# A post-norm transformer layer on eight cores: the context tile is copied out of PSUM ahead of its normalisation, and the down-projection weights are loaded from another queue

## The chip, the cores and the metric

One Trainium2 chip, all 8 cores, one launch. The cores do not exchange data. Each core owns 2048 of the 16384 tokens, half a sequence. In attention it takes four of the sixteen heads' weights and one batch after another (a batch is a wave), with the queries of its half and all 4096 keys. The metric is device time in microseconds (us) of the slowest core; less is better. TensorE (PE), VectorE (DVE), ScalarE (ACT), GpSimd (POOL) and SyncE (SP) are the engines. PE's clock has two levels, 1.2 and 2.4 GHz; a granted clock of 1.00 in a row is 2.4 GHz and 0.50 is 1.2 GHz.

## The reference

```python
x = L0_attn_query                                # [4, 4096, 2048] f32
x = layernorm(x + attention(x, Wqkv, Wproj, bproj))
x = layernorm(x + ffn(x, gate_up_packed, gate_up_scales, down_packed, down_scales))

# attention: 16 heads of 128, the sequence read as 16 groups (b*nh), softmax over keys
mixed = x @ Wqkv.T;  attn = softmax(q @ k.T / sqrt(128));  ctx = attn @ v;  out = ctx @ Wproj.T + bproj
# ffn: weights are 4-bit codes, eight in an int32, with a scale per 128 inputs
gate, up = split(x @ dequant(gate_up).T);  h = silu(gate) * up        # 5632 wide
y = h @ dequant(down).T;  y / sqrt(mean(y*y) + 1e-6)
```

## The kernel before

Every engine has its own instruction stream. The same Python walks through the whole program five times, once per engine, and emits only that engine's instructions; semaphores with counts worked out beforehand order them. So an instruction's place in its engine's stream follows from its place in the Python text, and a wait holds up all that stands behind it in that stream.

**Phase A** (to about 3650 us) runs four waves. A wave first makes K, V and Q for its tokens (L496, L514, L550), then does attention for four head slots. A slot has four query chunks of 512 queries. A query chunk walks over 32 key tiles in 16 pairs: PE makes two score tiles (`emit_S`, L587), ACT takes their exponential (L613), and PE multiplies them with V (L634) into two PSUM banks, `pCV[0]` and `pCV[1]`. Each bank holds two query tiles of 129 columns, the 129th being the sum of the exponentials. There is only this one pair of banks for the context, so the first V matmul of the next query chunk (`p == 0`) has to wait until the last one is out of them. DVE takes the reciprocals (L652, two instructions) and then writes `ctxg` by four multiplications (L663); POOL stores `ctxg` (L673). PE's wait at L627 is for the fourth of these multiplications.

Between these steps stand calls of `pace()`, twice in a query chunk: in its middle and between its last V matmul and the context work on DVE. Each adds one or two items of dequantisation: POOL loads packed weights (L285), DVE unpacks (L318, L324, L333) and scales them (L344), PE transposes (L365), ACT copies (L375), and POOL stores the bf16 weights to DRAM (L390). DVE is two items ahead of PE in this.

**Phase B** does the output projection and the first layer norm.

**Phase C** (from about 4400 us) runs over 4 chunks of 512 tokens. A chunk first does 44 gate and up steps (L966, L972), each on 1 MB of weights `wbC` loaded by SP (L947) into four buffers, with the chunk's 2 MB of input `h1tc` loaded by SP ahead of them (L935). Then come two passes (`pp`) of the down projection, each over 256 tokens: 44 steps (`ic`) of 8 matmuls (L1040) on 512 KB of weights `wdC`, again in four buffers. A pass ends with the second norm for its two token tiles on DVE (L1057 to L1136), and POOL stores each tile (L1145).

SP's stream in a chunk is: `h1tc`; 44 loads of `wbC`, each waiting for the step four before it; then for each pass two loads of `h1r` (L1008), of which the one for token tile t waits for the finished norm of tile t-2 (`cyt`, L1007). POOL's stream is: for each pass 44 loads of `wdC` (L1020), each waiting for the step four before it, then the two stores of the output, each waiting for its tile's finished norm. So POOL's `wdC` loads for the second pass stand behind the stores of the first.

Of the kernel before, what the change touches and what calls it, by code (L numbers as in the profile page):

```python
# [8 lines left out]
F32 = mybir.dt.float32  # L9
# [102 lines left out]
def build_nc(cfg):  # L112
# [56 lines left out]
    with contextlib.ExitStack() as TOP:  # L169
# [66 lines left out]
        with contextlib.ExitStack() as SA:  # L236
# [8 lines left out]
            Pt = EA(nc.sbuf_tensor("Pt", [128, 4, QCH], BF16))  # L245
            ctxg = [EA(nc.sbuf_tensor(f"ctxg{i}", [128, QT, 128], BF16)) for i in range(2)]
            rcp = EA(nc.sbuf_tensor("rcp", [128, 4], F32))
            sqb = EA(nc.sbuf_tensor("sqb", [128, 2, 128], BF16))
            bscal = EA(nc.sbuf_tensor("bscal", [1, 8], F32))
            bscal_bf = EA(nc.sbuf_tensor("bscal_bf", [1, 1], BF16))  # L250
# [146 lines left out]
            def phaseA(w: W):  # L397
# [44 lines left out]
                def pace(final=False):  # L442
                    us[0] += 1
                    tgt = n_items if final else us[0] * n_items // TOTAL_US
                    deq_vec_upto(min(n_items, tgt + DEQ_FIFO - 1))
                    deq_pe_upto(tgt)
# [24 lines left out]
                for wav in range(4):  # L471
# [98 lines left out]
                    for l in range(NL):  # L570
# [23 lines left out]
                        for qc in range(NQCH):  # L594
                            gqc = slot_idx * NQCH + qc
                            for p in range(NPt):
# [26 lines left out]
                                if w.on("tensor"):  # L623
                                    t = w.eng
                                    t.wait_ge(sems["sSP"], w.c("sSP"))
                                    if p == 0:
                                        t.wait_ge(sems["sCv"], w.c("sCv"))  # L627
                                    for tloc in range(2):
                                        ti = 2 * p + tloc
                                        inst = None  # L630
                                        for qt in range(QT):
                                            bank = pCV[qt // 2]
                                            off = (qt % 2) * 129
                                            inst = t.matmul(bank[:, off:off + 129],  # L634
                                                            Pt[:, (gpi % 2) * 2 + tloc,
                                                               qt * 128:(qt + 1) * 128],
                                                            V_wave[:, l, ti, 0:129],
                                                            start=(ti == 0), stop=(ti == KT - 1),
                                                            skip_group_check=True)
                                        w.inc(inst, "sPV", 1)  # L640
                                else:
                                    w.note("sPV", 2)
                            pace()
                            if w.on("vector"):
                                v = w.eng
                                v.wait_ge(sems["sPV"], w.c("sPV"))
                                if gqc >= 2:
                                    w.pwait("sCd", gqc - 2)
                                v.wait_ge(sems["sCv"], w.c("sCv"))
                                for b2 in range(min(2, QT)):  # L650
                                    nq = min(2, QT - 2 * b2)
                                    w.inc(v.reciprocal(  # L652
                                        out=rcp[:, b2 * 2:b2 * 2 + nq],
                                        in_=pCV[b2][:, 128:128 + 129 * nq:129]), "sCv", 1)
                                v.wait_ge(sems["sCv"], w.c("sCv"))
                            else:
                                w.note("sCv", min(2, QT))
                            for qt in range(QT):
                                bank = pCV[qt // 2]
                                off = (qt % 2) * 129  # L660
                                if w.on("vector"):
                                    v = w.eng
                                    w.inc(v.tensor_scalar(out=ctxg[gqc % 2][:, qt, :],  # L663
                                                          in0=bank[:, off:off + 128],
                                                          scalar1=rcp[:, qt:qt + 1], scalar2=None,
                                                          op0=ALU.mult), "sCv", 1)
                                else:
                                    w.note("sCv", 1)
# [234 lines left out]
        with contextlib.ExitStack() as SC:  # L903
# [15 lines left out]
            def phaseC(w: W):  # L919
# [10 lines left out]
                for ch in range(NTC):  # L930
# [69 lines left out]
                    for pp in range(NPAIR):  # L1000
# [12 lines left out]
                        for ic in range(ITC):  # L1013
                            kd = (ch * NPAIR + pp) * ITC + ic
                            par = ic % 4
                            if w.on("gpsimd"):
                                gp = w.eng
                                if kd >= 4:
                                    gp.wait_ge(sems["sDm"], w.m(f"dm{kd-4}", "sDm"))
                                w.pinc(gp.dma_start(out=wdC[par][:],  # L1020
                                                    in_=d_wdn[ic * 128:(ic + 1) * 128, :]),
                                       "sDw", kd, 4)
                            else:
                                w.pnote("sDw", kd, 4)
# [200 lines left out]
```

## Time and profile before

| | us |
|---|---|
| median of 2 runs | 6830.76 |
| lowest, highest run | 6687.31, 6974.21 |
| profiled execution | 6665.64 |
| its span, slowest core (core 1) | 6664.0 |
| spans of the eight cores | 6625.4 to 6664.0 |
| PE busy, share of the span | 4675.4, 70% |
| DVE busy | 2361.9, 35% |
| ACT busy | 2039.8, 31% |
| POOL busy | 612.8, 9% |

The profiled execution is one run; the two timed runs lie 21.7 and 308.6 us above it. A busy share is an average over phases that have different limits, so it doesn't say what a step is worth; for that one looks at what each stretch of idle PE time waited for.

### The profile page before, as it was taken

To read this page: it belongs to the slowest core of one execution; us is meant where nothing else is said; L and a number is where in the kernel's file an instruction comes from. 1 tells how busy PE (TensorE), PEld (TensorE's weight loads), DVE (VectorE), ACT (ScalarE), POOL (GpSimd) and SP (SyncE) were. 2 spreads that over 40 slices of the span, in tenths; PEclk is the share of its full clock that TensorE was granted. 3 is DMA by queue.
4 is the path that set the end of the run, shared out by engine and by line. 5 is a ranking of instruction groups with operands and counts; after the bars stand their busy time and mean duration, and the time that the engine had idled before them with its cause. 6 is when DMAs were issued, how large, how long until landed. Compare 5 with 4: busy or idle time off the path is not lost.

```text
span 6664.0 us, 82502 instructions; the slowest of 8 cores (6625.4 to 6664.0 us)
## 1 busy us (share of the span) xinstructions
PE 4675.4 (70%) x27520; PEld 2294.3 (34%) x27520; DVE 2361.9 (35%) x9935; ACT 2039.8 (31%) x2442; POOL 612.8 (9%) x862
## 2 busy tenths in 40 slices
PE   0576667876668766787666244469869969968994
PEld 0233443334433344433443122234324423423432
DVE  1234775337763466723665111110120012111002
ACT  0234665346653367633675011110000000000000
POOL 0000111001110011100111000000110010011011
PEclk9988898988989888898998577789989989989997
DMA  2333112341123411133111322244574575566455
GB/s 67 100 92 98 39 42 65 91 113 40 38 60 92 113 44 38 54 90 100 33 35 50 132 80 76 76 133 152 183 227 158 165 237 166 158 196 208 153 188 177
DMA packets 281821, 725.90 MB, mean 109 GB/s; under 512 B 26689, under 2 KB 43457, under 8 KB 271169
## 3 DMA queue, kind: packets, MB, share of 16 engines
q1 hardware_dynamic: 191618, 390.80, 19.9%
q0 software_dynamic: 89792, 329.84, 15.8%
q8 instruction: 231, 3.78, 0.2%
q14 instruction: 180, 1.47, 0.1%
HBM read 600.99 MB, written 119.54 MB: 108 GB/s over the span
## 4 chain that ended last, share of the span: by engine, by line
PE 44%; DMA 23%; DVE 14%; ACT 11%; issue 6%; POOL 1%; DVEq 0%; ACTq 0%; SPq 0%; POOLq 0%
DMA xf<-xt 10%; PE pC L966 9%; PE pC L972 9%; DMA wdC<-wdn_scr 6%; ACT Pt L613 5%; PE pC L1040 5%; PE pCV L634 5%; PE pCV L514 4%; PE pB L815 4%; PE pS L550 3%; PE pS L587 3%; DVE dqf L344 3%; ACT xbf L466 2%; DVE dq_bits L333 2%; DMA wq_st<-wqkvT 2%
## 5 line engine op out<-in xcount | busy, mean ns | idle before, releaser
L613 ACT ACTIVATE Pt<-pS,bias_c 128x1024 bf16<-128x1024 f32 x1024 | 1100.0, 1115 | 369.8 <-PE pS L587 356.9
L634 PE MATMUL pCV<-V_wave,Pt 128*128 128x129 bf16 x8192 | 705.0, 234 | 576.6 <-ACT Pt L613 316.3
L634 PEld LDWEIGHTS pCV<-V_wave,Pt 128*128 128x128 bf16 x8192 | 551.8, 105 | 1050.9 <-issue 1046.0
L1040 PE MATMUL pC<-wdC,hffnT 128*128 128x512 bf16 x2816 | 651.0, 387 | 269.4 <-DMA wdC<-wdn_scr 260.7
L514 PE MATMUL pCV<-wq_bf,xbf 128*128 128x512 bf16 x2048 | 517.3, 417 | 326.9 <-ACT V_wave L527 326.9
L966 PE MATMUL pC<-h1tc,wbC 128*128 128x512 bf16 x2816 | 649.7, 385 | 75.2 <-DVE hffnT L994 38.4
L587 PE MATMUL pS<-Q_wave,K_wave 128*128 128x512 bf16 x2048 | 674.3, 415 | 9.6 <-ACT K_wave L539 9.6
L344 DVE TENSOR_SCALAR dqf<-dq_bits,scf 128x128 bf16<-128x128 f32 x2112 | 667.5, 653 | 30.3 <-DVE dq_bits L333 1.4
L972 PE MATMUL pC<-h1tc,wbC 128*128 128x512 bf16 x2816 | 636.5, 379 | 0.0
L496 PE MATMUL pS<-xbf,wq_bf 128*128 128x512 bf16 x2048 | 453.9, 381 | 230.4 <-ACT xbf L466 220.3
L994 DVE TENSOR_TENSOR hffnT<-sGC,pC 128x512 bf16<-128x512 bf16 x176 | 121.0, 687 | 1107.5 <-ACT sGC L985 1107.5
L333 DVE TENSOR_TENSOR dq_bits<-dq_bits,dq_tmpB 128x128 int32<-128x128 int32 (+1 forms) x2176 | 479.9, 282 | 59.1 <-DVE dq_tmpB L324 1.8
L466 ACT CAST xbf<-xf 128x512 bf16<-128x512 f32 x512 | 313.9, 621 | 586.4 <-DMA xf<-xt 585.3
L1040 PEld LDWEIGHTS pC<-wdC,hffnT 128*128 128x128 bf16 x2816 | 268.5, 99 | 651.9 <-issue 371.8
L318 DVE TENSOR_SCALAR dq_bits<-pk 128x128 int32<-128x128 int32 (+1 forms) x2176 | 355.8, 235 | 338.5 <-PE pTq L365 298.5
L985 ACT ACTIVATE sGC<-pC 128x512 bf16<-128x512 f32 x176 | 105.1, 597 | 1076.9 <-PE pC L972 1073.9
L514 PEld LDWEIGHTS pCV<-wq_bf,xbf 128*128 128x128 bf16 x2048 | 212.6, 106 | 617.5 <-issue 428.1
L966 PEld LDWEIGHTS pC<-h1tc,wbC 128*128 128x128 bf16 x2816 | 278.3, 99 | 418.9 <-issue 96.0
L972 PEld LDWEIGHTS pC<-h1tc,wbC 128*128 128x128 bf16 x2816 | 275.5, 98 | 332.3
L390 POOL DMA_DIRECT2D wgu_scr<-wtile x176 | 180.2, 1025 | 2176.5 <-ACT wtile L375 2062.2
L496 PEld LDWEIGHTS pS<-xbf,wq_bf 128*128 128x128 bf16 x2048 | 199.7, 98 | 471.9 <-issue 240.9
L1020 POOL DMA_DIRECT2D wdC<-wdn_scr x352 | 185.9, 529 | 1769.3 <-PE pC L1040 1757.5
(74 smaller groups left out, 2881.2 us busy)
## 6 DMA issues: line engine op xcount, KB each, us to landing
wdC<-wdn_scr POOLq DMA_DIRECT2D x352, 512.0 KB, 5.0
xf<-xt SPq DMA_DIRECT2D x512, 256.0 KB, 2.8
wgu_scr<-wtile POOLq DMA_DIRECT2D x176, 256.0 KB, 3.5
wdn_scr<-wtile POOLq DMA_DIRECT2D x80, 256.0 KB, 3.5
wp_st<-wprojT SPq DMA_DIRECT2D x16, 1024.0 KB, 4.8
xr<-xrows SPq DMA_DIRECT2D x16, 1024.0 KB, 6.7
h_scr<-h1f POOLq DMA_DIRECT2D x16, 1024.0 KB, 8.8
h1rC<-h_scr SPq DMA_DIRECT2D x16, 1024.0 KB, 8.3
```

Of the source, the lines that this page charges most:

```text
L318: lastw = v.tensor_scalar(out=bits_view(j), in0=pkt[:, c0:c0 + ncols], scalar1=m8, scalar2=28 - 4 * j, op0=ALU.bitwise_and, op1=ALU.logica ...
L333: last_or = v.tensor_tensor(out=bits_view(j), in0=bits_view(j), in1=dq_tmpB[:, jj * ncols:(jj + 1) * ncols], op=ALU.bitwise_or)
L344: last = v.tensor_scalar(out=dq_f[fifo][:, g * 128:(g + 1) * 128] .rearrange("p (i e) -> p e i", e=8), in0=bits3[:, :, g * 16:(g + 1) * 16 ...
L466: w.inc(sc.copy(out=xbf[xslot][:, hc, :], in_=xf32[:, kx % 2, :]), "sXC", 1)
L496: inst = t.matmul(pK(l), wq_bf[:, hc, (NL + l) * 128:(NL + l + 1) * 128], xbf[slot][:, hc, :], start=(hc == 0), stop=(hc == HC - 1))
L514: inst = t.matmul(pCV[st % 2][:, 0:NL * 128], xbf[slot][:, hc, st * 128:(st + 1) * 128], wq_bf[:, hc, 2 * NL * 128:3 * NL * 128], start=(h ...
L587: w.inc(t.matmul(pS2[(gti // 2) % 2][:, (gti % 2) * 512:(gti % 2) * 512 + QCH], K_wave[:, l, ti * 128:(ti + 1) * 128], Q_wave[:, l, sqc * ...
L613: w.inc(sc.activation(out=Pt[:, (gpi % 2) * 2:(gpi % 2) * 2 + 2, :], in_=pin, func=AF.Exp, bias=bias_c[:, 0:1], scale=NORM), "sSP", 1)
L634: inst = t.matmul(bank[:, off:off + 129], Pt[:, (gpi % 2) * 2 + tloc, qt * 128:(qt + 1) * 128], V_wave[:, l, ti, 0:129], start=(ti == 0), ...
L966: t.matmul(gb[:, 0:TOKCH], wbC[par][:, hc, 0:128], h1tc[ch % 2][:, hc, :], start=(hc == 0), stop=(hc == HC - 1))
L972: inst = t.matmul(ub[:, 0:TOKCH], wbC[par][:, hc, 128:256], h1tc[ch % 2][:, hc, :], start=(hc == 0), stop=(hc == HC - 1))
L1040: inst = t.matmul(pC[tt2 * 4 + oc][:, 0:OCW], lhs, wdC[par][:, oc * OCW:(oc + 1) * OCW], start=(ic == 0), stop=(ic == ITC - 1))
```

## The change

In phase A the context is now copied as it is from PSUM to a new SBUF tile `ctx_sb` (two copies of 258 columns), and reciprocals and multiplications read that tile. PE's wait ahead of the first V matmul of a query chunk is for the two copies of the chunk before (`ctxev`), no longer for the multiplications. In phase C the `wdC` loads are issued by SP in place of POOL, at the same place of the Python text and with the same waits. So in SP's stream they stand behind the pass's two `h1r` loads, and the next chunk's `h1tc` and first `wbC` loads stand behind the 44 `wdC` loads of the second pass.

```diff
+            ctx_sb = EA(nc.sbuf_tensor("ctx_sb", [128, 2, 258], F32))
...
-                                    if p == 0:
-                                        t.wait_ge(sems["sCv"], w.c("sCv"))
+                                    if p == 0 and gqc >= 1:
+                                        t.wait_ge(sems["sCv"],
+                                                  w.m(f"ctxev{gqc-1}", "sCv"))
...
                             pace()
+                            nbk = max(1, QT // 2)
...
-                                for b2 in range(min(2, QT)):
+                                for b2 in range(nbk):
+                                    wq2 = min(2, QT - 2 * b2)
+                                    w.inc(v.tensor_copy(out=ctx_sb[:, b2, 0:129 * wq2],
+                                                        in_=pCV[b2][:, 0:129 * wq2]),
+                                          "sCv", 1)
...
+                            w.snap(f"ctxev{gqc}", "sCv")
...
                                     w.inc(v.reciprocal(
                                         out=rcp[:, b2 * 2:b2 * 2 + nq],
-                                        in_=pCV[b2][:, 128:128 + 129 * nq:129]), "sCv", 1)
+                                        in_=ctx_sb[:, b2, 128:129 + 129 * (nq - 1):129]),
+                                        "sCv", 1)
...
                                     w.inc(v.tensor_scalar(out=ctxg[gqc % 2][:, qt, :],
-                                                          in0=bank[:, off:off + 128],
+                                                          in0=ctx_sb[:, qt // 2, off:off + 128],
...
-                            if w.on("gpsimd"):
-                                gp = w.eng
+                            if w.on("sync"):
+                                s = w.eng
                                 if kd >= 4:
-                                    gp.wait_ge(sems["sDm"], w.m(f"dm{kd-4}", "sDm"))
-                                w.pinc(gp.dma_start(out=wdC[par][:],
-                                                    in_=d_wdn[ic * 128:(ic + 1) * 128, :]),
+                                    s.wait_ge(sems["sDm"], w.m(f"dm{kd-4}", "sDm"))
+                                w.pinc(s.dma_start(out=wdC[par][:],
+                                                   in_=d_wdn[ic * 128:(ic + 1) * 128, :]),
                                        "sDw", kd, 4)
```

## Rows read from the trace of the kernel before

**Rows 1.** The page, costliest groups: busy, mean ns | idle before, releaser.
```profile
L1040 PE MATMUL pC<-wdC,hffnT 128*128 128x512 bf16 x2816 | 651.0, 387 | 269.4 <-DMA wdC<-wdn_scr 260.7
```

**Rows 2.** The view of waits: us in total, times, longest.
```profile
PE pCV L634 <- DVE ctxg L663: 256.1, 48, 11.3
DVE rcp L652 <- PE pCV L634: 64.3, 14, 7.2
```

**Rows 3.** Timeline, end of a query chunk (start, us taken, instruction, idle before it).
```profile
808.86 0.40 DVE L652 RECIPROCAL rcp<-pCV 128x2 f32<-128x2 f32 x2
...
809.41 1.12 DVE L663 TENSOR_SCALAR ctxg<-pCV,rcp 128x128 bf16<-128x128 f32 x4 [0.15 <-DVE rcp L652]
...
810.68 0.50 PE L634 MATMUL pCV<-V_wave,Pt 128*128 128x129 bf16 x6 [2.39 <-DVE ctxg L663]
```

**Rows 4.** Timeline, the same place where DVE was early, and the last short wait.
```profile
726.52 0.73 PE L634 MATMUL pCV<-V_wave,Pt 128*128 128x129 bf16 x6 [1.99 <-ACT Pt L613]
...
3589.40 0.62 PE L634 MATMUL pCV<-V_wave,Pt 128*128 128x129 bf16 x8 [2.39 <-DVE ctxg L663]
```

**Rows 5.** Groups with shapes kept apart, and timeline of four 512-wide copies.
```profile
L663 DVE TENSOR_SCALAR ctxg<-pCV,rcp 128x128 bf16<-128x128 f32 x256 | 72.1, 344 | 9.5 <-DVE rcp L652 8.0
L1057 DVE COPY yC<-pC 128x512 f32<-128x512 f32 x64 | 39.7, 682 | 793.5 <-PE pC L1040 793.5
...
4818.41 2.48 DVE L1057 COPY yC<-pC 128x512 f32<-128x512 f32 x4 [85.27 <-PE pC L1040]
```

**Rows 6.** Timeline, DVE after one context: idle until the next packed weights are there.
```profile
685.09 0.17 DVE L300 TENSOR_SCALAR scf<-scb 128x16 f32<-128x16 f16 x1 [10.13 <-DMA pk<-gup]
```

**Rows 7.** Timeline, from the first to the second pass of chunk 0.
```profile
4847.29 1.35 DVE L1136 TENSOR_SCALAR outfC<-r2C,aggC,scaC 128x2048 f32<-128x2048 f32 x1
...
4849.08 0.42 SPq L935 DMA_DIRECT2D h1tc<-h1T_scr  x1
...
4849.73 2.10 POOL L1020 DMA_DIRECT2D wdC<-wdn_scr  x4
4862.27 8.10 PE L1040 MATMUL pC<-wdC,hffnT 128*128 128x512 bf16 x26 [43.97 <-DMA wdC<-wdn_scr]
```

**Rows 8.** Timeline, PE at the same place in chunks 1 to 3.
```profile
5420.32 2.29 PE L1040 MATMUL pC<-wdC,hffnT 128*128 128x512 bf16 x5 [44.58 <-DMA wdC<-wdn_scr]
...
5978.23 2.29 PE L1040 MATMUL pC<-wdC,hffnT 128*128 128x512 bf16 x5 [46.88 <-DMA wdC<-wdn_scr]
...
6534.18 3.15 PE L1040 MATMUL pC<-wdC,hffnT 128*128 128x512 bf16 x7 [42.58 <-DMA wdC<-wdn_scr]
```

**Rows 9.** Stretches: us, PE, PEld, DVE, ACT, POOL busy, PEclk, DMA share, GB/s.
```profile
4862.00:4964.00 102.00, 85.96 (x352) 33.85 (x352) 0.10 (x1) 0.00 (x0) 21.13 (x40) 0.91 0.84 275
...
5420.00:5520.00 100.00, 83.65 (x352) 34.31 (x352) 0.00 (x0) 0.00 (x0) 21.13 (x40) 0.93 0.85 280
...
5978.00:6081.00 103.00, 85.44 (x352) 34.51 (x352) 0.00 (x0) 0.00 (x0) 21.14 (x40) 0.91 0.83 269
...
6534.00:6622.00 88.00, 80.94 (x352) 33.69 (x352) 0.00 (x0) 0.00 (x0) 21.16 (x40) 0.97 0.76 250
```

**Rows 10.** Timeline, from the second pass of chunk 0 into chunk 1, PE alone.
```profile
4961.84 1.89 PE L1040 MATMUL pC<-wdC,hffnT 128*128 128x512 bf16 x8
...
4966.53 4.80 PE L966 MATMUL pC<-h1tc,wbC 128*128 128x512 bf16 x15 [2.81 <-DVE yC L1057]
...
4994.13 2.29 PE L966 MATMUL pC<-h1tc,wbC 128*128 128x512 bf16 x5 [12.21 <-DVE hffnT L994]
```

**Rows 11.** Timeline, the start of phase C.
```profile
4403.88 0.38 SPq L935 DMA_DIRECT2D h1tc<-h1T_scr  x1
...
4425.08 2.29 PE L966 MATMUL pC<-h1tc,wbC 128*128 128x512 bf16 x5 [28.37 <-DMA wbC<-wgu_scr]
```

**Rows 12.** DMA issues: KB each, median us from issue to landing.
```profile
wdC<-wdn_scr POOLq DMA_DIRECT2D x352, 512.0 KB, 5.0
xf<-xt SPq DMA_DIRECT2D x512, 256.0 KB, 2.8
```

More of the change, by code:

```diff
@@ L649, in phaseA @@
                                 v.wait_ge(sems["sCv"], w.c("sCv"))
-                                for b2 in range(min(2, QT)):
+                                for b2 in range(nbk):
[3 more added lines that the diff above has]
+                                          "sCv", 1)
+                            else:
+                                w.note("sCv", nbk)
+                            w.snap(f"ctxev{gqc}", "sCv")
+                            if w.on("vector"):
+                                v = w.eng
+                                v.wait_ge(sems["sCv"], w.c("sCv"))
+                                for b2 in range(nbk):
                                     nq = min(2, QT - 2 * b2)
@@ L653, in phaseA @@
                                         out=rcp[:, b2 * 2:b2 * 2 + nq],
-                                        in_=pCV[b2][:, 128:128 + 129 * nq:129]), "sCv", 1)
+                                        in_=ctx_sb[:, b2, 128:129 + 129 * (nq - 1):129]),
+                                        "sCv", 1)
                                 v.wait_ge(sems["sCv"], w.c("sCv"))
                             else:
-                                w.note("sCv", min(2, QT))
+                                w.note("sCv", nbk)
                             for qt in range(QT):
-                                bank = pCV[qt // 2]
                                 off = (qt % 2) * 129
```

## The prediction

> **What bounds the kernel now.** I read the page first. PE is busy for 70% of the span and no other engine for more than 35%, so the time is PE's own work plus what PE waits for, and only waits of PE that the change touches can pay. The costliest groups show one of the two: the down projection's matmuls had 260.7 us of idle PE time ahead of them that ended with a `wdC` load [rows 1]. The view of waits shows the other: PE waited 256.1 us, 48 times, for the context multiplications, on average 5.3 us, while DVE waited for PE's last V matmul only 14 times out of 64 query chunks [rows 2]. In the other 50 DVE was late. The timeline of one such place tells why: DVE comes out of a dequantisation item that `pace()` put ahead of the context work, and takes its reciprocals at 808.86 without having been idle [rows 3]. So most of the 5.3 us is dequantisation, which the change leaves where it is. What it can shorten is the last part, from the first reciprocal to PE's next V matmul: 808.86 to 810.68, 1.82 us [rows 3].
>
> For phase C I took the timeline around the long waits and the stretches. Each chunk has one wait of 43 to 47 us between its two passes [rows 7, 8], 178.0 us in all, and 82.7 of the 260.7 us lie in the passes themselves. The long one is mostly the norm of two tiles on DVE: its last instruction starts at 4847.29, then SP and POOL are released together, at 4849.08 and 4849.73, and the first `wdC` lets PE go on at 4862.27 [rows 7].
>
> **Part 1, the context copy.** Removed from PE's path: two reciprocals and four multiplications, with the hand-over 1.82 us [rows 3]. Put on it: two PSUM copies of 258 columns. No such copy is in the trace. The nearest on both sides are 128 columns from PSUM, 344 ns, and 512 columns, 682 ns [rows 5]. Four in a row take 1.12 us at 128 columns [rows 3] and 2.48 at 512 [rows 5], so from start to start 0.26 and 0.60 us. Between them in proportion to the columns, a 258-wide copy takes 0.46 us and the next can start after 0.38. Two take 0.84 us, and the hand-over to PE 0.15 (810.68 less the end of the multiplications, 810.53 [rows 3]), together 0.98 against 1.82: 0.84 us saved where DVE is what PE waits for. If the copies cost as 128-wide ones do the saving is 1.07 us, if as 512-wide ones 0.39.
>
> PE can't go on sooner than its probabilities allow: where DVE was early, the gap was still 1.99 us, until ACT [rows 4]. So of the 48 waits those under 1.99 + 0.84 = 2.83 us gain only what lies above 1.99. There are 13 of them, the first and the last 2.39 us long [rows 3, 4], 0.40 us gained each. Sum: 35 x 0.84 + 13 x 0.40 = 34.6, taken as **-35 us**. With the other two copy prices it is 35 x 0.39 + 13 x 0.3, some 18 us, or 35 x 1.07 + 13 x 0.4, some 43.
>
> The copies are extra work on DVE. Behind the release come the same six instructions as before, at no more than their 1.67 us, so a query chunk costs DVE up to 0.84 us more and `ctxg` is finished up to 0.84 us later against DVE's start. I cost this at nothing: DVE then idles until the next packed weights land, 10.13 us in the case shown [rows 6]. POOL's `ctxg` store and the weight load behind it are late by the same amount against DVE, but PE is earlier. Without that cover 64 x 0.84 = 54 us of DVE work would lie on the path and eat the gain.
>
> **Part 2, the `wdC` loads on SP.** The long wait stays. SP's stream has the `h1r` load of the second pass's second tile ahead of the `wdC` loads, and it waits for the same finished norm for which POOL's store waited. What changes is what travels beside them. In chunks 0 to 2 SP sent `h1tc` (2 MB) and four `wbC` loads (4 MB) at the same moment as POOL the first `wdC` [rows 7]; now these come 44 loads later. Chunk 3 has no next chunk and shows the price without them: a long wait of 42.58 us against 43.97, 44.58 and 46.88 [rows 7, 8], so 1.4 + 2.0 + 4.3 = 7.7 us; and a second pass of 88 us with a granted clock of 0.97, against 102, 100 and 103 us at 0.91 to 0.93 [rows 9], so 14 + 12 + 15 = 41 us. Together **-48 us**, with room for 10 us either way, since the clock recovered differently in each.
>
> What is late next is the start of the next chunk. SP issues its last `wdC` when step 39 is done, four steps of 1.89 us [rows 10] before the pass ends at E; `h1tc` follows some 0.4 us later, at E - 7.2. At the start of phase C the same `h1tc` and `wbC` loads went out with up to four `wdC` loads in flight, and PE went on 21.2 us after the first issue, 4403.88 to 4425.08 [rows 11]. So PE starts the chunk at E + 14.0 where it started at E + 2.8 [rows 10]. But this chunk had a second wait: its third step needs DVE, which is still in the norm. From E = 4963.73 (the last eight matmuls start at 4961.84 and take 1.89) to that step at 4994.13 are 30.4 us, of which 12.21 idle, so the two steps before it took 27.6 - 12.2 = 15.4 us [rows 10]. [...] The lateness falls into the wait for DVE: 0.7 us at each of three places, **+2 us**.
>
> The issue itself: POOL leaves 352 instructions, SP takes them, and before the gate and up steps end it has nothing else to wait for, so the first pass finds its four loads landed as it does now. Whether a load lands sooner or later from SP the trace can't show for this form; I take no difference, and treat both directions as rivals.
>
> **Sum.** -35 - 48 + 2 = -81 us on the profiled execution's 6665.64, 6585. The median of the two runs shown lies 165 us above that execution, and these two differ by 287 us; taken off the median, 6830.76 - 81 = 6750. That is 1.2%. I call 2% about what a measurement of this kernel can tell from no change.
>
> **Rivals.**
> *Loads land sooner from SP* (chance 0.13). 256 KB took 2.8 us from SP, 512 KB took 5.0 from POOL [rows 12]; the size explains part of it. A load is needed three steps after its issue, 3 x 1.89 = 5.7 us, so landings of 5.0 cause the short waits in the passes. Of the 41 us in part 2, 12 are PE busy time at the lower clock (85.96, 83.65 and 85.44 against 80.94 [rows 9]), so 29 are waits. 82.7 less these leaves 54 us as the most that can go; half gives 6750 - 27 = 6723. The Trainium skill, DMA: Bandwidth & Descriptors, Specifications, gives a first-byte latency of about 1 us for GpSimd's path and about 0.6 for SyncE's. By that, each of the some 90 short waits would shrink by up to 0.4 us, an estimated 36 us; no run so far shows it. The same page (Issuing engines are not separate DMA queues) says that all of them run on the same 16 DMA engines whichever engine issues, which speaks against any gain in rate.
> *The next chunk starts late* (0.12). Beside traffic, `h1tc` and `wbC` may take longer than at the start of phase C. For each us beyond E + 14 at which PE starts, three are lost. With 14 us more at each place part 2 gives -48 + 42, and the time is 6750 + 40 = 6790. Against it: no `wdC` load is issued any more once `h1tc` is.
> *The context gain is eaten* (0.10). DVE's added 0.84 us comes back where DVE has little idle time between two contexts, or the late packed weights push the next item over PE's wait. Then only part 2 is left: 6830.76 - 46 = 6785.
> *Slower: `wdC` lands late from SP* (0.05). With four buffers a step takes a quarter of landing and use, (L + 1.89)/4. At L = 5.0 that is 1.72, below PE's 1.89. From L = 5.7 the load sets the pace, from 6.6 the gain of 81 us is gone (0.23 us on each of 352 steps), from 8.1 it is 2% slower than before; at L = 7.5 the time is 6750 + 352 x 0.46 = 6912. Against it: SP's 256 KB in 2.8 us [rows 12].
> The forecast itself has 0.60.
>
> **Range.** Down: 54 us of short waits and 8 of cheaper copies more, from the lower of two runs that stand 143 us below their median, since a median of two may fall on either; 6585 covers both in part. Up: the late chunk start, the eaten gain, and no gain at all, 6850. Faster by over 2% would need 133 us, nearly all of the upper bounds at once: 0.10. Slower by over 2% needs the slow landings: 0.05. Within 2%: 0.85.
>
> **What the changed profile would show.** Part 1: PE's wait now named by the new copy, again about 48 times, near 220 us; copies of about 0.46 us. Part 2: the long wait still there four times at 41 to 43 us, second passes of chunks 0 to 2 at 87 to 90 us as in chunk 3; `h1tc` issued about 7 us before the pass ends, PE idle some 14 us at the chunk's start on `wbC`, and the 12 us wait for `hffnT` gone or under 2 us. Wrong if the wait on the copy stays at 256 us, if the second passes stay above 95 us, or if PE's idle time at the chunk's start exceeds 20 us. Landing of `wdC` from SP under 4.5 us speaks for the first rival, above 5.7 for the last.

## The result and the profile after

The changed kernel is 2.0% faster: the ratio of its time to that of the kernel before is 0.980, with a 95% interval of 0.977 to 0.983, so the gain is clear, and on which side of 2% it lies is not. Its profiled execution took 6539.33 us, with 6536.5 us for the slowest core (core 6), against 6665.64 and 6664.0. I had forecast 81 us less than the profiled 6665.64; it is 126 us less. The plain medians, 6888.89 us over 11 runs after and 6683.14 over 10 runs before, can't be compared, since many executions of either kernel, more of them after, fell into a slow state in which the cores of one die or both ran at a lower granted clock, and the ratio leaves these out.

To see where the time went, I took from the timeline of each of the eight cores when each part begins and ends. Means over the cores, in us:

| part | before | after | difference | forecast |
|---|---|---|---|---|
| four attention waves | 1820.1 | 1795.1 | -25.0 | -35 |
| phase C, four first passes | 344.8 | 322.3 | -22.5 | 0 |
| second passes of chunks 0 to 2 | 302.8 | 252.1 | -50.7 | -41 |
| second pass of chunk 3 | 88.1 | 82.8 | -5.3 | 0 |
| gate and up part of chunk 0, and the four steps from gate and up to down | 313.3 | 313.2 | -0.1 | 0 |
| four long waits between passes | 173.1 | 164.9 | -8.2 | -8 |
| end of a second pass to end of the next gate and up part, three times | 968.4 | 968.1 | -0.3 | +2 |
| last matmul to the end | 41.8 | 36.8 | -5.0 | 0 |
| from the last wave to the start of phase C's matmuls | 779.2 | 772.9 | -6.3 | 0 |
| rest of phase A | 1818.8 | 1810.9 | -7.9 | 0 |
| all | 6650.3 | 6519.1 | -131.2 | -81 |

The 7.9 us in the rest of phase A can't be put down to the change: in the runs below whose code there is that of one or the other kernel, its first piece alone (start to first wave) lies anywhere between 614 and 635 us. The attention waves of these runs agree within 3 us, so small effects are read from the parts and not from whole times.

The context chain. The view of waits, PE, for the slowest core after (what waited <- for what: us in total, times, longest), answering [rows 2]:

```profile
PE pCV L636 <- DVE ctx_sb L655: 206.3, 39, 10.5
PE pC L1054 <- DMA wdC<-wdn_scr: 192.6, 60, 42.0
PE pC L980 <- DMA wbC<-wgu_scr: 37.9, 3, 21.7
```

The wait for DVE carries the copy's name now, and it is still 206 us: the dequantisation item ahead of the context work was not touched. The wait for `wdC` fell from 260.7 us in 99 pieces to 192.6 in 60. The timeline of one end of a query chunk, core 1, answering [rows 3]:

```profile
661.70 0.96 DVE L655 COPY ctx_sb<-pCV 128x258 f32<-128x258 f32 x2
662.76 0.23 DVE L666 RECIPROCAL rcp<-ctx_sb 128x2 f32<-128x2 f32 x2
662.81 0.76 PE L636 MATMUL pCV<-V_wave,Pt 128*128 128x129 bf16 x8 [2.50 <-DVE ctx_sb L655]
663.10 0.87 DVE L677 TENSOR_SCALAR ctxg<-ctx_sb,rcp 128x128 bf16<-128x128 f32 x4
```

And the groups with shapes kept apart, slowest core, answering [rows 5]:

```profile
L655 DVE COPY ctx_sb<-pCV 128x258 f32<-128x258 f32 x128 | 58.7, 501 | 50.5 <-PE pCV L636 50.5
```

From the first copy to PE's next V matmul it is 1.11 us (661.70 to 662.81) where it was 1.82. DVE is at it until 663.97, 2.27 us in place of 1.67. Means over the eight cores of all that PE waits ahead of its V matmuls (L634, now L636): for DVE 252.2 us before and 207.6 after, for ACT 316.4 and 336.0. So of the 45 us that left the wait for DVE, 20 stand now as waits for ACT's exponentials, and 25 are gone.

The passes. Stretches of the slowest core after, one for each pass (us, busy time of PE, PEld, DVE, ACT, POOL, PEclk, DMA share, GB/s): first and second pass of chunk 0, then of chunk 3, answering [rows 9]:

```profile
4702.00:4780.00 78.00, 75.79 (x338) 32.54 (x343) 0.00 (x0) 0.00 (x0) 0.00 (x0) 1.00 0.81 270
4821.00:4908.00 87.00, 79.64 (x345) 34.05 (x352) 0.21 (x1) 0.00 (x0) 0.00 (x0) 0.97 0.83 271
...
6296.00:6376.00 80.00, 75.55 (x338) 32.52 (x342) 0.31 (x1) 0.00 (x0) 0.00 (x0) 1.00 0.80 263
6416.00:6500.00 84.00, 79.16 (x345) 34.05 (x352) 0.07 (x1) 0.00 (x0) 0.00 (x0) 0.97 0.81 266
```

The stretches of the first passes leave out their first 1.7 and 1.9 us. On this core a first pass takes 80 to 81 us, where core 1 before took 85 to 87, and the clock in it is 1.00: short waits are gone. The second pass of chunk 0 shrinks from 102 to 86 and now resembles that of chunk 3. Between passes and into the next chunk, timeline of the same core, answering [rows 7, 10]:

```profile
4811.01 0.55 POOL L1159 DMA_DIRECT2D out<-outfC  x1 [13.85 <-DVE outfC L1150]
4811.25 2.35 SPq L1034 DMA_DIRECT2D wdC<-wdn_scr  x4
4821.87 1.01 PE L1054 MATMUL pC<-wdC,hffnT 128*128 128x512 bf16 x2 [41.76 <-DMA wdC<-wdn_scr]
...
4900.62 0.92 SPq L949 DMA_DIRECT2D h1tc<-h1T_scr  x1
...
4905.73 1.89 PE L1054 MATMUL pC<-wdC,hffnT 128*128 128x512 bf16 x8 [0.16 <-DMA wdC<-wdn_scr]
4915.27 1.01 PE L980 MATMUL pC<-h1tc,wbC 128*128 128x512 bf16 x2 [7.66 <-DMA wbC<-wgu_scr]
...
4937.93 1.44 PE L980 MATMUL pC<-h1tc,wbC 128*128 128x512 bf16 x3 [6.87 <-DVE hffnT L1008]
```

The long wait is there as before, 41.76 us. `h1tc` goes out at 4900.62, 7.0 us before the pass ends at 4907.62, and PE goes on 7.66 us after that end; the third step still waits for DVE, 6.87 us in place of 12.21. As forecast, the one wait took from the other.

### The profile page after: what moved, and what is told of

Its sections match the earlier page's. It is cut to its first block, busy times and chain, and to the rows that moved or that the text cites. A ratio compares the mean times of both kernels' runs of the same rounds, so it can differ in the third digit from the quotient of the medians.

```text
span 6536.5 us, 82171 instructions; the slowest of 8 cores (6505.8 to 6536.5 us)
## 1 busy us (share of the span) xinstructions
PE 4624.5 (71%) x26998; PEld 2295.7 (35%) x27520; DVE 2398.3 (37%) x10063; ACT 2038.0 (31%) x2442; POOL 433.0 (7%) x510
## 4 chain that ended last, share of the span: by engine, by line
PE 46%; DMA 22%; DVE 14%; ACT 11%; issue 6%; POOL 0%; ACTq 0%; DVEq 0%; SPq 0%; another core or an unknown queue 0%; POOLq 0%
DMA xf<-xt 11%; PE pC L980 9%; PE pC L986 9%; PE pC L1054 6%; ACT Pt L614 5%; PE pCV L636 5%; PE pCV L515 5%; DMA wdC<-wdn_scr 5%; PE pB L829 4%; PE pS L551 3%; PE pS L588 3%; DVE dqf L345 3%; ACT xbf L467 2%; DMA wq_st<-wqkvT 2%; DVE dq_bits L334 2%
## 5 line engine op out<-in xcount | busy, mean ns | idle before, releaser
L636 PE MATMUL pCV<-V_wave,Pt 128*128 128x129 bf16 x8192 | 706.0, 235 | 551.2 <-ACT Pt L614 337.7
L636 PEld LDWEIGHTS pCV<-V_wave,Pt 128*128 128x128 bf16 x8192 | 552.2, 105 | 1026.0 <-issue 1022.0
L1054 PE MATMUL pC<-wdC,hffnT 128*128 128x512 bf16 x2760 | 628.2, 383 | 204.5 <-DMA wdC<-wdn_scr 192.6
L588 PE MATMUL pS<-Q_wave,K_wave 128*128 128x512 bf16 x1838 | 625.3, 417 | 25.5 <-ACT K_wave L540 10.0
L980 PEld LDWEIGHTS pC<-h1tc,wbC 128*128 128x128 bf16 x2816 | 278.5, 99 | 409.5 <-issue 87.3
L325 DVE TENSOR_SCALAR dq_tmpB<-pk 128x128 int32<-128x128 int32 (+1 forms) x2176 | 347.6, 228 | 0.0
L301 DVE TENSOR_SCALAR scf<-scb 128x16 f32<-128x16 f16 x88 | 15.9, 181 | 883.6 <-DMA pk<-gup 667.8
```

Source lines behind the costliest of these rows:

```text
L588: w.inc(t.matmul(pS2[(gti // 2) % 2][:, (gti % 2) * 512:(gti % 2) * 512 + QCH], K_wave[:, l, ti * 128:(ti + 1) * 128], Q_wave[:, l, sqc * ...
L636: inst = t.matmul(bank[:, off:off + 129], Pt[:, (gpi % 2) * 2 + tloc, qt * 128:(qt + 1) * 128], V_wave[:, l, ti, 0:129], start=(ti == 0), ...
L980: t.matmul(gb[:, 0:TOKCH], wbC[par][:, hc, 0:128], h1tc[ch % 2][:, hc, :], start=(hc == 0), stop=(hc == HC - 1))
L1054: inst = t.matmul(pC[tt2 * 4 + oc][:, 0:OCW], lhs, wdC[par][:, oc * OCW:(oc + 1) * OCW], start=(ic == 0), stop=(ic == ITC - 1))
```

## Experiments

Eleven kernels ran, one of them twice. All ratios are to the kernel before. Theory A for the 50 us beyond the forecast was, after the two traces: SyncE issues a `wdC` load sooner after the step that frees its buffer than GpSimd does. Counted over all steps from the eighth of each pass on, the median from the next step's first weight load to the issue is 0.80 us for GpSimd before and 0.45 for SyncE after (core 1 of each). The timelines show single cases, before and after:

```profile
6548.14 1.89 PE L1040 MATMUL pC<-wdC,hffnT 128*128 128x512 bf16 x8 [0.81 <-DMA wdC<-wdn_scr]
...
6550.56 0.53 POOL L1020 DMA_DIRECT2D wdC<-wdn_scr  x1 [2.17 <-PE pC L1040]
```

```profile
4844.72 0.81 PE L1054 MATMUL pC<-wdC,hffnT 128*128 128x512 bf16 x3
4845.60 0.32 SPq L1034 DMA_DIRECT2D wdC<-wdn_scr  x1
```

A step's matmuls end at 6550.03 and GpSimd issues 0.53 us later; they end at 4845.53 and SyncE issues 0.07 later. Over all those steps (core 1 of each) the medians of this time are 0.54 and 0.08 us. The rivals were that the queue moves the data faster, and that all comes from deferring the next chunk's loads.

### The two halves apart

Only the context change (the `wdC` loads stay on GpSimd), and only the `wdC` loads:

```diff
-                            if w.on("sync"):
-                                s = w.eng
+                            if w.on("gpsimd"):
+                                gp = w.eng
...
-                                w.pinc(s.dma_start(out=wdC[par][:],
...
+                                w.pinc(gp.dma_start(out=wdC[par][:],
...
```

This is the edit of the changed kernel for the first; the second is the kernel before with the last hunk of the change alone.

> The context change alone, with the wdC loads still issued by GpSimd. Theory A (the two changes add up, and the context part is worth what the attention waves of the changed kernel show): the four attention waves take 1795 us together in place of 1820 (means over the cores), phase C stays as before (first passes about 86 us, second passes of chunks 0 to 2 about 101, tail after the last matmul 41.8), and the time falls by 25 to 35 us, 0.4 to 0.5%. Theory B (the context change is worth nothing, and the attention gain seen belongs to other differences between two executions): no change within 0.2%. GpSimd's last drain stays at 7.7 us in both.

> The wdC loads on SyncE alone, the context chain as before. Theory A: phase C as in the changed kernel (first passes 80 to 81 us, second passes 83 to 85, long waits 41 us each, tail 36.8), attention waves 1820 us as before; the time falls by 95 to 105 us, 1.4 to 1.6%. GpSimd's last drain falls to 2.7 us. Theory B (the prediction's sizing holds and the rest came with the context change): 46 us, first passes still 86 us, drain still 7.7.

Measured: the context half 0.996 (0.992 to 1.000), the load half 0.985 (0.981 to 0.989). Their product is 0.981, the whole change 0.980. By the parts the two add up within 1 us: attention waves 1795.5 us with the context half and 1819.5 with the load half (1795.1 with both, 1820.1 with none); first passes 86.1 and 80.6; second passes of chunks 0 to 2 84.3 with the load half; last matmul to the end 41.7 and 36.8. Theory A holds in both. So the context half is worth 25 us and the load half 90 to 100.

### Only the deferral

```diff
                         if ch >= 2:
                             s.wait_ge(sems["sCg"], w.m(f"cgc{ch-2}", "sCg"))
+                        if ch >= 1:
+                            s.wait_ge(sems["sDm"],
+                                      w.m(f"dm{ch * NPAIR * ITC - 5}", "sDm"))
```

> The kernel before with one wait more on SyncE: the next chunk's h1tc and wbC loads wait until step 39 of the chunk's second pass, so they go out when they do in the changed kernel, while wdC stays with GpSimd. Theory A (deferring this traffic is one half, SyncE's earlier issue of wdC the other): second passes of chunks 0 to 2 fall from 101 to 88 us, as chunk 3's, first passes stay at 86, the tail stays at 41.8, long waits fall by some 2 to 3 us in chunks 0 to 2; in all 40 to 50 us faster, 0.6 to 0.75%. Theory B (all of phase C's gain is the deferral): 95 us. Theory C (it is all the queue): no change.

> The same kernel as the earlier one with only the deferral, for a profile whose clock is undisturbed. Theory A: second passes of chunks 0 to 2 at 88 us (101 before), first passes at 86, long waits of chunks 0 to 2 shorter by 2 to 3 us, chunk starts as in the changed kernel, tail 41.8. If the second passes come out at 83 us, the issue from SyncE has no part in them and only in the first passes.

Measured: 0.994 (0.991 to 0.997), 40 us, the time that theory A gave. The parts are means over cores 0 to 3 of the second run's profile, whose granted clock (0.886 to 0.889) is that of the kernel before. First passes 85.7 us, second passes of chunks 0 to 2 92.0, that of chunk 3 87.4, the end 41.8. First and second pass of chunk 0, core 0, stretches as above:

```profile
4713.00:4800.00 87.00, 77.70 (x345) 33.06 (x350) 0.66 (x2) 0.00 (x0) 21.24 (x40) 1.00 0.73 242
4841.00:4932.00 91.00, 80.76 (x345) 33.45 (x350) 0.65 (x2) 0.00 (x0) 21.24 (x40) 0.97 0.80 266
```

The first pass is what it was. The deferral takes 9 us off each second pass (100.9 to 92.0), not 13: it does not reach chunk 3's 88. The other 8 us down to 84.0 come only with the loads on SyncE, and they have two parts. The first forty steps take 81.3 us here and 76.2 in the changed kernel, 5.1 us, much as in a first pass. The last four, when `h1tc` is on its way, take 10.8 us here and 7.9 in the changed kernel. At the next chunk's start PE is held up 4.3 us here and 7.3 in the changed kernel. I read both as `h1tc` travelling beside the pass's last `wdC` loads, where on one queue it stands behind them: the pass's end gains 3 us, and the 3 us that the next chunk starts later fall into its wait for DVE, for up to the end of the next gate and up part the two kernels take the same (968.5 and 968.1 us for the three).

### The loads on a third engine

```diff
-                            if w.on("gpsimd"):
-                                gp = w.eng
+                            if w.on("scalar"):
+                                s = w.eng
...
```

> The kernel before with the wdC loads issued by ScalarE: they leave GpSimd, but are not put in front of SyncE's next h1tc and wbC loads. Theory A (the issue is later on GpSimd than on another engine): first passes fall from 86 to about 80 us after their start, the last second pass to 83, the tail to 36.8 us; the second passes of chunks 0 to 2 stay disturbed, 93 to 98 us. Each first pass starts some 4 to 5 us later, since its first loads stand behind the last Silu, and each second pass some 1.5 us sooner. In all 20 to 45 us faster. Theory C (the gain is only that nothing else travels beside wdC): first passes stay at 86 us, second ones at 101, and the late start makes it 15 us slower.

Measured: 0.994 (0.991 to 0.997). First passes 83.2 us, the last second pass 87.3, second passes of chunks 0 to 2 104.9, the end 36.8. The median issue is as early as on SyncE (0.46 us, core 4). Faster first passes and the short end are theory A's, but 83.2 is not 80, and the second passes that share the way with `h1tc` and `wbC` got worse, not better; why, no run here tells. A first pass starts 2.4 us later, not 4 to 5. What I had not expected is how short the long waits of chunks 0 to 2 are: 33.5 us in place of 43.7. Core 4:

```profile
4830.90 1.78 ACTq L1020 DMA_DIRECT2D wdC<-wdn_scr  x4
4832.83 0.32 SPq L1008 DMA_DIRECT2D h1rC<-h_scr  x1
...
4835.48 1.87 PE L1040 MATMUL pC<-wdC,hffnT 128*128 128x512 bf16 x4 [33.06 <-DMA wdC<-wdn_scr]
```

ScalarE's loads stand behind its last square root, 1.9 us ahead of `h1r`, and the first lands in 4.5 us. In the kernel before the same load took 12 us, from 4849.73 to 4862 [rows 7], beside the `h1r` load, the stores, `h1tc` and `wbC`. Where `h1tc` and `wbC` don't travel, it takes 9.8 us on average (chunk 3 before, and 9.6 to 10.0 in all chunks of the changed kernel), so of the 7.5 us some 2 are theirs and some 5 those of the `h1r` load and the stores. With the 2 us of lead itself that makes the 10 us that a long wait lost.

### A fifth buffer, before and after

```diff
-            wdC = [EC(nc.sbuf_tensor(f"wdC{i}", [128, H], BF16)) for i in range(4)]
+            wdC = [EC(nc.sbuf_tensor(f"wdC{i}", [128, H], BF16)) for i in range(5)]
...
-                            par = ic % 4
+                            par = kd % 5
...
-                                if kd >= 4:
+                                if kd >= 5:
...
```

> The kernel before (wdC on GpSimd) with five wdC buffers in place of four. Theory A (the short waits in a pass come from issue and landing together taking longer than three steps of 1.73 us, 5.2 us; so 0.35 us of issue on SyncE and one more buffer here are two ways to the same slack): first passes fall from 86 to 77 to 79 us, second passes of chunks 0 to 2 from 101 to 88 to 95, the last second pass from 88 to 80; long waits and the tail of 41.8 us stay; in all 45 to 70 us faster. Theory B (the transfers are limited by rate, and SyncE's queue moves them faster): first passes stay at 84 us or more.

> The changed kernel with five wdC buffers. Theory A: the rest of the short waits goes, first passes from 80.6 to 77 to 78 us, second passes from 83.5 to 79 to 81; the chunk starts, long waits and tail stay; 18 to 28 us faster than the changed kernel. Theory B (by rate): no change.

Measured: the kernel before with five buffers 0.991 (0.989 to 0.993), the changed one with five 0.974 (0.972 to 0.976). First passes 77.4 us from 86.2, and 76.2 from 80.6; last second passes 79.0 and 78.1. One pass of the kernel before with five buffers, core 1:

```profile
4691.00:4768.00 77.00, 76.29 (x352) 34.29 (x352) 0.41 (x1) 0.00 (x0) 20.61 (x39) 1.00 0.77 266
```

GpSimd's loads carry 266 GB/s in a pass whose only wait is one of 1.7 us for DVE at its start. In a first pass the rate was no limit: theory B falls for both. The waits came from issue and landing together against three steps. The second passes of chunks 0 to 2 are another matter: with five buffers they fell to 94.0 us in the kernel before and to 78.6 in the changed one. Beside the next chunk's loads a fifth buffer is not enough; there the deferral counts.

### The issue made late again

```diff
                                 if kd >= 4:
-                                    s.wait_ge(sems["sDm"], w.m(f"dm{kd-4}", "sDm"))
+                                    for _ in range(8):
+                                        s.wait_ge(sems["sDm"], w.m(f"dm{kd-4}", "sDm"))
```

> The changed kernel with SyncE's wait ahead of each wdC load repeated seven times more, which does nothing but let the load go out some 0.3 us later (a satisfied wait takes SyncE about 0.045 us). Theory A (the first passes got faster because SyncE issues a load 0.35 us sooner after the step that frees its buffer): first passes go back from 80.6 to 85 or 86 us, the last second pass from 83 to 87 or 88, the others likewise by 4 to 5. Theory B (the queue that carries the loads makes the difference, not their time of issue): first passes stay below 82 us. The tail stays at 36.8 us.

The profile is read on cores 4 to 7, whose granted clock (0.887 to 0.889) is that of the kernels compared; there is no ratio. The issue is at 0.81 us from the next step's first weight load, where GpSimd's median was 0.80. That median hides a difference, since in GpSimd's kernel PE waited more often ahead of the next step. From the end of the step's matmuls it is 0.43 us here, 0.08 in the changed kernel and 0.54 for GpSimd, so the issue is still 0.11 us earlier than GpSimd's. One case, core 7 (matmuls end at 4700.48, issue at 4700.91):

```profile
4699.67 0.81 PE L1055 MATMUL pC<-wdC,hffnT 128*128 128x512 bf16 x3
4700.91 0.32 SPq L1035 DMA_DIRECT2D wdC<-wdn_scr  x1
```

First passes 82.8 us (80.5 on the same cores of the changed kernel), the last second pass 87.2 (83.2), the others 86.2 (84.2), the end 36.7. First pass of chunk 0 on core 7, as a stretch:

```profile
4677.00:4759.00 82.00, 77.80 (x352) 33.25 (x352) 0.09 (x1) 0.00 (x0) 0.00 (x0) 1.00 0.78 257
```

Neither theory has it alone. On these four cores the late issue brings back 2.3 of the 5.5 us of a first pass (86.0 before) and 4.0 of the 5.0 us of the last second pass (88.2 before). Some 3 us of a first pass are not brought back. By the same rate, 2.3 us for 0.35, the missing 0.11 us of issue are an estimated 0.7 of them; some 2.5 us stay with GpSimd's loads. Their median from issue to landing in the first passes is 4.97 to 5.08 us before and 4.79 to 4.87 here. What part of that is the length of the issue instruction (0.53 us against 0.32) and what its way to the DMA engines, no run here tells apart.

### Every second load on GpSimd

```diff
-                            if w.on("sync"):
+                            if w.on("gpsimd" if ic % 2 else "sync"):
...
```

> The changed kernel with every second wdC load issued by GpSimd, the others by SyncE. Theory A (the short waits go with the later issue on GpSimd): about half of the difference between GpSimd's 86 us and SyncE's 80.6, first passes 82 to 84 us; the next chunk's loads are still deferred, so second passes of 85 to 87. For the tail: GpSimd's last drain takes 7.66 us after 858 DMA instructions and 2.68 after 506; with 682 it takes 5.2 us if it grows in proportion to their number, and 7.7 us if it is a matter of whether GpSimd loads are used late in the program at all.

Measured in one profiled execution: first passes 85.2 us, second passes 91.6, the last one 91.4. Half of the difference was expected; in the first passes 4.6 of the 5.6 us came back. The last pass came out above the kernel before's 88.1, but it lies anywhere between 86.9 and 101.4 us on the eight cores (85.7 to 91.2 before), so that it is slower than with GpSimd alone is not shown. On core 4 SyncE's loads of the first passes landed 4.88 us after the next step's first weight load, GpSimd's 5.56, medians. So with two queues SyncE's loads came sooner than in the changed kernel (5.22) and since PE takes them in turn, a load that comes sooner gains nothing while the other is late. With four buffers and every second load on GpSimd, two of the buffers are always filled by GpSimd, and I read their pace as that of the pass; with that reading nearly the whole difference, and not half of it, is what was to be expected. The Trainium skill's page DMA: Bandwidth & Descriptors (Queues, rings and completion order) has each DMA engine go round the queues it has work for, a packet from each. In this run every `wdC` load landed after the one issued before it, on all eight cores, so the trace doesn't show that such turns cost anything here. The end took 42.1 us.

### What is left: the order on DVE and on SyncE

The remaining wait of PE for DVE, with the context work ahead of `pace()`; and the long wait, with `h1r` loaded by GpSimd:

```diff
-                            pace()
                             nbk = max(1, QT // 2)
...
+                            pace()
                             n2 = slot_idx
```

```diff
-                            if w.on("sync"):
+                            if w.on("gpsimd"):
                                 s = w.eng
                                 if tt_abs >= 2:
                                     s.wait_ge(sems["sCy"], w.m(f"cyt{tt_abs-2}", "sCy"))
                                 w.pinc(s.dma_start(out=h1r[parq][:],
...
```

> The changed kernel with DVE's whole context work (copies, reciprocals, multiplications) moved ahead of the dequantisation items that stand before it, nothing else. Theory A (what is left of PE's wait for DVE, 206 us in 39 waits of the changed kernel's slowest core, is the dequantisation item ahead of the context work): these waits go down to ACT's floor of about 2 us, so some 40 x 3.1 = 125 us go, and up to 30 more where the clock no longer falls; attention waves 1795 -> 1640 to 1680 us, 6380 us for the slowest core. Theory B (DVE is short of time in attention, so the wait only moves to PE's transposes): waves fall by less than 50 us and PE waits for dqf. The first passes and all of phase C stay as in the changed kernel.

> The changed kernel with the two h1r loads of a pass issued by GpSimd, so that SyncE's wdC loads stand behind no wait for the norm. Theory A (the long wait of 41 us between the passes is SyncE's wait for the norm of the pass before, plus landing): it falls to the time until DVE has evicted the second tile, 18 to 19 us, four times, 85 to 92 us faster than the changed kernel, 6440 us for the slowest core. GpSimd's last drain rises slightly, to about 2.9 us, if it grows in proportion to the DMAs it issued. Theory B (PE waits for the norm itself): long waits stay at 41 us.

The first: 0.969 (0.966 to 0.971), attention waves 1706.2 us, 89 less, between the two theories. The view of waits of its slowest core shows why:

```profile
PE pCV L636 <- ACT Pt L614: 389.2, 505, 2.5
...
PE pTq L366 <- DVE dqf L345: 114.6, 16, 10.0
PE pCV L636 <- DVE ctxg L676: 6.0, 3, 2.0
```

The wait for the context went from 206 us to 6, and 115 us in 16 waits came up at PE's transposes (10 us before), and the waits for ACT's exponentials grew from 338 to 389 us: the item that had stood ahead is late now. So the item ahead of the context was the cause, as the prediction read it, and it was only partly free to move.

The second: 0.972 (0.970 to 0.974). Timeline of core 0 at the first change of passes, PE:

```profile
4772.55 10.78 PE L1054 MATMUL pC<-wdC,hffnT 128*128 128x512 bf16 x40 [18.45 <-DVE yC L1071]
4783.77 6.99 PE L1054 MATMUL pC<-wdC,hffnT 128*128 128x512 bf16 x31 [0.44 <-DMA wdC<-wdn_scr]
4794.72 5.53 PE L1054 MATMUL pC<-wdC,hffnT 128*128 128x512 bf16 x12 [3.97 <-DMA wdC<-wdn_scr]
```

The long wait is 18.45 us and ends with the eviction of the second tile, as theory A has it. Of the 23 us won each time some 8 come back as short waits in the second pass (92.0 us in place of 84.0), as I read it since `h1r`, the stores and `wdC` now travel while PE works: the two passes and the wait between take 190.7 us together, 205.5 in the changed kernel.

### All together

The changed kernel with both orders, five buffers and both tiles of a pass evicted (into two `yC` tiles) before their norms:

> The changed kernel with what the other runs point to: context work ahead of the dequantisation items, h1r loads on GpSimd, five wdC buffers, and both tiles of a pass evicted into two yC tiles before their norms. If the parts add up: attention waves 1706 us, long waits 5.2 us in place of 41 (less up to 6 us each that comes back as short waits beside h1r and the stores), passes 77 to 80 us; 6250 to 6300 us for the slowest core. Rival: DVE's norm of a pass now runs beside the next pass and the passes slow down by their DMA traffic, so that the gain from the long waits is under 100 us; then 6320 or more.

Its slowest core took 6316.7 us, its profiled execution 6318.43, its fastest run 6304.09 beside 6640.34 for the fastest run of the kernel before on the same chip, about 5% less; there is no interval. Waves 1705 us, two passes with their wait 170.8 us. It lies just above the range in which the parts add up, and just below the rival's 6320. What the rival names did happen: the long waits fell from 41.2 to 5.1 us, but a second pass takes 89.5 us where the changed kernel with five buffers takes 78.5, so of 144 us won at the waits some 100 are left.

## Why the prediction was wrong

- **What bounds the kernel**: right. The two waits read from [rows 1, 2] are the ones that shrank, and the reading that most of the 5.3 us was dequantisation was shown by moving the context ahead of it.
- **The context copy**: right in kind, sized too high, -35 against -25 us. Two copies and the hand-over took 1.11 us, not 0.98, so 0.71 us and not 0.84 are saved where DVE is what PE waits for; 35 x 0.71 + 13 x 0.40 gives 30. The last 5 us I can't place. The DVE work that I had covered with idle time is 0.60 us per query chunk (2.27 less 1.67; DVE's busy time rose by 36.4 us, from 2361.9 to 2398.3); it may cost a little, but no run here showed it.
- **Deferred traffic**: right in kind, too large in what I gave it. Chunk 3's pass as a price was near, but the deferral alone brings 9 us a pass, not 13. The whole -50.7 us contains 5 us a pass that belong to the failed step below, and 3 us a pass from the one queue, on which `h1tc` stands behind the last `wdC` loads. The 7.7 us for the long waits came out at 8.2, in part by luck: 46.88 us was one core's wait, and the means before, 43.7 us in chunks 0 to 2 against 42.0 in chunk 3, would have given 5. After the change all four fell to 41.2, chunk 3's too.
- **Start of the next chunk**: the trade between the two waits was right (+2 forecast, -0.3 measured). The 0.7 us at each of the three places is a term that no run shows; they came out 0.1 us shorter each. The load time was too long: PE went on 14.3 to 15.5 us after the issue of `h1tc` (core 6), not 21.2. At the start of phase C [rows 11] the first `wdC` loads had been sharing the way, and core 1 was the slowest there of cores that took 16.0 to 21.2. That start got shorter too: PE's idle time ahead of its first matmul there fell from 25.7 us to 19.9 (means over the cores), most of the 6.3 us in the table that I had not seen at all. It follows what GpSimd sends at that moment: 19.5 and 19.9 us where the `wdC` loads are SyncE's or ScalarE's, 25.3 with the context half alone, and 25.5 where GpSimd sends the `h1r` loads.
- **The failed step**: "Whether a load lands sooner or later from SP the trace can't show for this form; I take no difference, and treat both directions as rivals." I looked at the time from issue to landing, and it really stayed at 5.0 us. What I left out is the time from the end of a step to the issue. The trace of before showed it: GpSimd's load went out 0.54 us after PE's matmuls had ended, and SyncE's `wbC` loads in the same trace 0.14 us after (medians, core 1). I had also put a step at 1.89 us, which is the time of its eight matmuls from the first start to the last end; from start to start it is 1.73. Three steps are then 5.2 us, not 5.7, and a landing of 5.0 leaves 0.2 us for the issue, so that 0.54 or 0.08 us decides whether PE waits. First passes and the last second pass gave 27.8 us by it and by what else GpSimd's loads cost, for which I had put nothing either; with 5 us in each of the other second passes it is some 43 us. The 3 us each that the one queue gives at their ends make it about 50, as much as lies between forecast and result. The other errors nearly cancel: 10 us too much for the context and 14 for the deferral on one side; 5 us at the end, 6 at the start of phase C and 8 that are no effect of the change on the other; that they nearly cancel is luck. My first rival had the sign and, with half of 54 us, half of the size, though not the cause, since the median landing on the page did not move; I gave it 0.13.
- **The end**: 5 us that I had not in mind, below.
- **The rivals**: a late chunk start and an eaten context gain did not come. The slow landing on SyncE did not either.

## What to carry to other kernels

With a fixed number of buffers, what a load must beat is the whole way from the step that frees the buffer to the step that needs the data: wait, issue and landing. Measure that sum on the engine that issues now and on the engine that would, and compare it with (buffers - 1) steps; in the first passes a fifth buffer gave more here than the other queue (8.8 us against 5.6), and both together 10. Over the whole kernel the other queue gave more (0.985 against 0.991), because it also puts the next chunk's loads behind the pass. When a wait hangs on an engine with its own long stream, read what stands ahead of the awaited instruction in the text: moving the context work ahead of the dequantisation was worth more than three times the shorter eviction (89 us against 25), and taking the norm's wait out of the weights' queue 15 us a chunk.

## What the runs showed of the hardware

- From a satisfied wait to the start of the DMA instruction GpSimd needs longer than SyncE or ScalarE: the median issue came at 0.80 us after the next step's first weights against 0.45 and 0.46. From the end of the step's matmuls it is 0.54 us for GpSimd and 0.08 for the other two. Its DMA instruction takes 0.53 us, SyncE's 0.32.
- GpSimd's closing drain is part of the program's time. The rows of before and after (start and length of the last drain, ns min/median/max):

```profile
L169 POOLq DRAIN  x1: 7659/7659/7659, 6656.1 to 6656.1; - x1
```

```profile
L169 POOLq DRAIN  x1: 2677/2677/2677, 6533.6 to 6533.6; - x1
```

  It took 7.66 us in every kernel with 858 DMA instructions on GpSimd, 2.68 with 506, 3.17 with 522 and 7.99 with 682, where every second `wdC` load was GpSimd's. So it does not grow in proportion to their number. It was long wherever GpSimd loaded weights in the last passes; whether that is the cause was not tried.
- With every second load on GpSimd, nearly all of SyncE's gain in a first pass was gone: 85.2 us, against 80.6 with SyncE alone and 86.2 with GpSimd alone (one profiled execution).
- Issued 0.43 us after the end of a step's matmuls, SyncE's loads kept PE waiting less than GpSimd's issued after 0.54: first passes 82.8 against 86.0 us on the same four cores. The 0.11 us are an estimated 0.7 us of that.
